# A four-layer graph network on one core: narrower one-hot groups, an integer addition moved to VectorE, and matrices placed inside a sum

## What is computed

```python
# 1: graph convolution: features = sum over edges of norm * (h @ W)[src]; then a small network
# 2: convolution with a matrix per edge
w = (relu(efeat @ W1 + b1) @ W2 + b2).reshape(E, 16, 16)
msg = einsum('ei,eio->eo', h[src], w)
agg = segment_sum(msg, dst) / max(deg, 1) + bias        # then relu and batch norm
# 3: sheaf layer: two Householder reflections per edge, messages to src and to dst
out = relu(x - sum_src(msg_s) - sum_dst(msg_d))
# 4: attention, 256 channels per edge
e1, e2 = (efeat @ W_msg + b_msg) * h[src], (efeat @ W_attn + b_attn) * h[src]
attn = softmax of e2 over the edges of one dst, per channel
ft = segment_sum(e1 * attn, dst).sum(axis=1)
```

## Time and profile before

| what | value |
|---|---|
| median of 3 runs | 9471.54 us (9471.53 to 9472.74) |
| the profiled execution: its time | 9465.25 us |
| the profiled execution: its span | 9463.5 us |
| mean granted clock of TensorE | 0.854 of 2.4 GHz |
| busy: TensorE, VectorE, GpSimd, ScalarE | 81%, 78%, 73%, 49% of the span |
| second convolution | about 1530 to 3270 us of the span |
| sheaf layer | about 3440 to 6025 us |
| attention | about 6135 to 9355 us |

### The profile page before, as it was taken

The page is one execution under the profiler, slowest core; times in us unless marked ns, Lnnn a source line. Parts: engine busy times, 40 slices in busy tenths (PEclk is TensorE's granted clock), DMA queues, the critical chain, the costliest instruction groups (busy, mean ns, idle before and its releaser), DMA issues. The chain is left out here.

```text
span 9463.5 us, 135509 instructions
## 1 busy us (share of the span) xinstructions
PE 7645.1 (81%) x35152; PEld 4283.9 (45%) x35152; DVE 7338.7 (78%) x11881; ACT 4606.7 (49%) x7496; POOL 6896.2 (73%) x6335
## 2 busy tenths in 40 slices
PE   3777774999999728888888888578888888888884
PEld 3666653555555415555555555333333333333331
DVE  6666653777777738888888888588888998988987
ACT  4666663667667416565655665323333333333333
POOL 6777776766666567777777777378777777777774
PEclk9888886777777659999999999789999999999997
DMA  4222211111111111111111111122222222222223
GB/s 147 55 52 53 55 46 36 42 41 40 42 41 40 34 17 32 31 27 31 31 27 31 31 31 21 18 62 72 77 72 71 72 71 75 75 71 72 71 74 99
DMA packets 498923, 493.19 MB, mean 52 GB/s; under 512 B 180303, under 2 KB 396134, under 8 KB 497959
## 3 DMA queue, kind: packets, MB, share of 16 engines
q1 hardware_dynamic: 298823, 371.60, 11.6%
q0 software_dynamic: 199904, 119.78, 9.1%
HBM read 240.96 MB, written 249.95 MB: 52 GB/s over the span
## 5 line engine op out<-in xcount | busy, mean ns | idle before, releaser
L2485 POOL DMA_INDIRECT attn_got<-tab,attn_line x1760 | 2152.3, 1223 | 648.7 <-issue 511.2
L1945 POOL DMA_INDIRECT sheaf_got<-tab,sheaf_idx x1612 | 1712.7, 1062 | 490.0 <-issue 472.5
L2538 PE MATMUL attn_q<-attn_X,ident 128*128 128x512 f32 x3520 | 1799.3, 658 | 1.8 <-DVE attn_X L2710 1.8
L2034 PE MATMUL sheaf_acc<-sheaf_hot_hi,sheaf_wide 128*128 128x392 bf16 x6696 | 1361.4, 346 | 272.1 <-DVE sheaf_hot_hi L2237 270.2
L1469 POOL DMA_INDIRECT nnconv_got<-tab,nnconv_idx x1116 | 1100.0, 986 | 456.0 <-issue 322.8
L1167 POOL DMA_INDIRECT gcn_got<-tab,gcn_idx x868 | 1018.9, 1174 | 301.4 <-issue 275.4
L2671 DVE TENSOR_TENSOR attn_T<-attn_w,attn_got 128x1024 f32<-128x1024 f32 x880 | 1035.0, 1218 | 246.4 <-PE attn_w L2529 206.6
L2538 PEld LDWEIGHTS attn_q<-attn_X,ident 128*128 128x128 f32 x3520 | 699.9, 210 | 1136.6 <-issue 1136.6
L2615 ACT COPY attn_S<-attn_q 128x512 f32<-128x512 f32 x440 | 255.9, 582 | 1624.4 <-PE attn_q L2545 1624.4
L2034 PEld LDWEIGHTS sheaf_acc<-sheaf_hot_hi,sheaf_wide 128*128 128x128 bf16 x6696 | 657.2, 106 | 809.2 <-issue 481.0
L2529 PE MATMUL attn_w<-src_hi 32*128 32x512 f32 x3520 | 586.5, 738 | 437.6 <-DVE attn_T L2671 436.7
(11 more groups left out here) (502 smaller groups left out, 13931.2 us busy)
## 6 DMA issues: line engine op xcount, KB each, us to landing
sums<-attn_S SPq DMA_DIRECT2D x110, 1024.0 KB, 4.2
tops<-attn_S SPq DMA_DIRECT2D x110, 512.0 KB, 2.9
attn_got<-tab,attn_line POOLq DMA_INDIRECT x1760, 2.6
sheaf_got<-tab,sheaf_idx POOLq DMA_INDIRECT x1612, 2.4
gcn_key<-src_key SPq DMA_DIRECT2D x62, 384.0 KB
gcn_blk<-src_blk SPq DMA_DIRECT2D x62, 384.0 KB
nnconv_got<-tab,nnconv_idx POOLq DMA_INDIRECT x1116, 2.4
nnconv_key<-src_key SPq DMA_DIRECT2D x62, 256.0 KB, 3.1
```

Of the source, the lines that this page charges most:

```text
L1945: e.indirect_dma_start(out=got[at.b][:, j, D:D + T2], out_offset=None, in_=tab[2], in_offset=indices(idx[at.b], j)).then_inc(s_got[half][a ...
L2034: mm = e.matmul(pacc[k][:, 0:HH], wide[at.b][half][:, part, col, :], hot[:, k * HH:(k + 1) * HH], start=False, stop=False, skip_group_chec ...
L2485: e.indirect_dma_start(out=got[at.b][:, 4 * q + n, :], out_offset=None, in_=tab[3], in_offset=indices(ids[:, q, n, :], D + 2)).then_inc(s_ ...
L2538: e.matmul(to, ident[:, :], X[:, q, :, n, :], start=n == 0, stop=False)
```

## The change

Three edits. In the second convolution the one-hot groups have GC = 3 columns instead of 4, so 6 columns come by one-hot and 20 are gathered, two more per block; all buffers, matmuls and copies of these groups are 384 instead of 512 wide, and each group picks 3 columns. The last part of the gathers is now columns 16 to 19. In the sheaf layer `ids_of` goes from GpSimd's program; VectorE adds the offset (NP times the mark) in `fixed`, behind each mark. In the attention TensorE issues the matrices of quad 0 two blocks ahead inside `quad_sum(at, 0)`, behind the third of the four positions. The diff, cut to its core:

```diff
@@ second convolution
         GN = 2
+        GC = 3
         BY_ACT = (NC, 4)
-        JN = J - GN * GW
+        JN = J - GN * GC
...
-            key = [sbl(f"key{b}", [P, GN, GW * P], F16) for b in range(2)]
-            blk = [sbl(f"blk{b}", [P, GN, GW * P], F16) for b in range(2)]
-            hot = [sbl(f"hot{q}", [P, NC, GW * P], F32R) for q in range(2)]
-            held = [sbl(f"held{q}", [P, GW * P]) for q in range(2)]
+            key = [sbl(f"key{b}", [P, GN, GC * P], F16) for b in range(2)]
+            blk = [sbl(f"blk{b}", [P, GN, GC * P], F16) for b in range(2)]
+            hot = [sbl(f"hot{q}", [P, NC, GC * P], F32R) for q in range(2)]
+            held = [sbl(f"held{q}", [P, GC * P]) for q in range(2)]
...
-                                mm = e.matmul(pacc[:, :],
+                                mm = e.matmul(pacc[:, 0:GC * P],
...
-                        for j in range(GW):
-                            at_col = q * GW * 2 * D + j * 2 * D
+                        for j in range(GC):
+                            at_col = q * GC * 2 * D + j * 2 * D
...
-                        e.copy(got[at.b][:, JN + g * GW:JN + (g + 1) * GW, :].rearrange("p j f -> p (j f)"),
-                               psel[:, q * GW * 2 * D:(q + 1) * GW * 2 * D]).then_inc(s_moved, 1)
+                        e.copy(got[at.b][:, JN + g * GC:JN + (g + 1) * GC, :].rearrange("p j f -> p (j f)"),
+                               psel[:, q * GC * 2 * D:(q + 1) * GC * 2 * D]).then_inc(s_moved, 1)
...
-                                               in1=pacc[:, :], op0=ALU.is_equal, op1=ALU.mult).then_inc(s_mask, 1)
+                                               in1=pacc[:, 0:GC * P], op0=ALU.is_equal, op1=ALU.mult).then_inc(s_mask, 1)
@@ sheaf layer, GpSimd
-                    def ids_of(at):
-                        turn_wait(e, s_ln[at.b], at.half(32 * NP2, 32 * NP2))
-                        for m in range(2):
-                            ids = line[at.b].bitcast(I32)[:, m, :, :, D + 2]
-                            e.tensor_tensor(ids, ids, void_src[:, bass.ds(at.of(2 * QB, m * QB), NP2), :],
-                                            ALU.add).then_inc(s_ids_part if m == 0 else s_ids, 1)
-
                     def step(at):
                         sources(at, 0)
-                        if 0 < at.k <= NBL:
-                            ids_of(at.plus(-1))
                         sources(at, 1)
@@ sheaf layer, VectorE
                         for m in range(2):
-                            e.tensor_copy(line[at.b][:, m, :, :, D + 1],
-                                          void[:, bass.ds(at.of(2 * QB, m * QB), NP2), :]).then_inc(s_mk, 1)
+                            quads_at = bass.ds(at.of(2 * QB, m * QB), NP2)
+                            ids = line[at.b].bitcast(I32)[:, m, :, :, D + 2]
+                            e.tensor_copy(line[at.b][:, m, :, :, D + 1], void[:, quads_at, :]).then_inc(s_mk, 1)
+                            e.scalar_tensor_tensor(out=ids, in0=void[:, quads_at, :], scalar=float(NP), in1=ids, op0=ALU.mult,
+                                                   op1=ALU.add).then_inc(s_ids_part if m == 0 else s_ids, 1)
@@ attention, TensorE
-                    def quad_sum(at, q):
+                    def quad_sum(at, q, between=None):
...
                         for n in range(4):
                             e.matmul(to, ident[:, :], X[:, q, :, n, :], start=n == 0, stop=False)
+                            if between and n == 2:
+                                between()
...
-                        quad_sum(at, 0)
-                        if at.k < NBQ - 2:
-                            matrices(at.plus(2), 0)
+                        quad_sum(at, 0, (lambda: matrices(at.plus(2), 0)) if at.k < NBQ - 2 else None)
```

## The result

The changed kernel takes 9229.65 us, the median of 3 runs (9218.75 to 9231.04), beside 9471.54 us before: a ratio of 0.9741, with a 95% interval of 0.9719 to 0.9763. That is 242 us faster. The forecast was 9246 us with a range of 9195 to 9350. The profiled execution has a span of 9227.9 us; it was 9463.5, so 235.6 us are to be found in the trace.

A forecast was written before the change was run, and what follows sets the result against it. Bounds: TensorE's chain in the convolution, GpSimd with VectorE just under it in the sheaf layer, VectorE's wait for matrices in the attention. Gains of 75 + 4 + 147 = 226 us from 9471.5 give 9246 us, range 9195 to 9350.

The forecast's parts named there:

- The block of 25.7 us: Second convolution: GpSimd's time per block after the change, twenty gathers at 1.275 us plus 0.2, making it the bound.
- 214 - 158: Second convolution: GpSimd's present waits, 214 us, less 158 us for two new gathers per block; a gain of 56 us.
- The lead: Second convolution: the last product starts 39 us after the last gather; this shrinks to some 15, 23 us more gain.
- reserve: Second convolution: ScalarE's 7.86 us of one-hot work lose up to 1.97, so TensorE's 1.54 us wait shrinks too; not counted.
- B: Rival: the convolution gains nothing, TensorE stays at its lower clock longer and remains the bound at 27.3 us; 9320, chance 0.14.
- D: Rival: slower, the clock never comes back in the convolution, 31.3 us per block against 27.3; 9568, chance 0.06.
- 24 x 0.34 = 8 us on the path: Sheaf layer: VectorE's added offsets cost 0.34 us in each of 24 blocks where it comes late out of the loop's turn.
- 0.53 us per block: Attention: VectorE's mean wait for TensorE's first matrices after the change, instead of 1.88 us.
- six take 5.0: Attention, slow block: six of eight TensorE records take 5.0 us before the moved matrices, which start at 8020.6.
- next limit: Attention: GpSimd's gathers, line fetches and what lies between, 3008 us or 27.34 per block, just below the forecast period of 27.6.
- Rival C: The attention gains little: TensorE is late with every later quad, or the clock falls there; up to 9392, chance 0.12.

The follow-up runs named there:

- version with the wait per quad: Changed kernel, but each attention product waits only for the product that read the same part of T two blocks before, not all four: 9211.84 us, ratio 0.9732.
- loaded version: The version with the wait per quad plus one idle GpSimd instruction (an iota) at the start of every attention block: 9237.98 us, ratio 0.9761.

## Why the prediction was right, and where its steps were off

The kernel is 242 us faster and the forecast had 226. Of the 16 us, 9 come from the three stages, 3 less than forecast in the convolution, 8 more in the sheaf layer and 4 more in the attention, 6 from the profiled execution of before, which lay under its median, and the rest from between the stages.

**Convolution, -75 against -72 (and -71 alone).** The reading was right: GpSimd held back, TensorE's chain the bound, and GpSimd the bound afterwards. Three details were not.

- The block of 25.7 us. "20 x 1.275 + 0.2" left out the 0.96 us between the copy of the indices and the first gather. Before, it ran inside GpSimd's waits for products and bias, and no row showed it. Instead of 56 us the end of the gathers moved by 41 (3227.6 to 3186.6). Both terms of "214 - 158" were off, in opposite directions. GpSimd's waits fell not by 214 us but from 220.7 to 60.2, which is all hand-over. And the new gathers cost not 158 us but 119: busy time rose from 1100.0 to 1184.2 and gaps from 322.8 to 358.0, as a gather takes 955 ns where it took 986. The difference, 160.5 - 119.4, is the 41 us.
- The lead. I had it shrink from 39 to 15 us; it shrank to 8 (3186.6 to 3194.4). So the two halves were 41 + 31 and not 56 + 19 to 23. That the sum comes so near is luck.
- Who waits. I named VectorE. It is ScalarE, whose bias copy is the first instruction that needs the last columns of a block, and TensorE behind it. ScalarE's 1.5 us less one-hot work (3.65 + 2.71 for 4.40 + 3.46) therefore did not shrink TensorE's idle time, my "reserve".

Rivals B and D did not come. The clock went from 0.75 to 0.73, and a selection and the matrices behind it still run at the lower level (1.49 and 2.08 us, where others of the same size take 0.85 and 1.13). But at 26.0 us per block TensorE still stands idle for 1.6 to 2.6 us. The Trainium skill ("TensorE: Matmul & The Clock Gate", Part 1) says that activity releases the throttle. The trace agrees: in the block above the slow sum takes 4.57 us, less than twice the 2.70 of the fast one, so the clock came back inside it, as it did before the change (5.90 against 3.53).

**Sheaf layer, -4 against -12 in the trace, and no difference alone.** VectorE's waits for gathers, 11.6 us, were the right thing to look for, and they are gone. From first to last message the three traces with the old layer (before, and the convolution and the attention alone) take 2521.6 to 2522.6 us, the eight with the new one 2504.8 to 2511.5. That is 10 to 18 us, so 11.6 was not the strict bound that it was taken for; what gives the rest was not followed up. The term that failed is "24 x 0.34 = 8 us on the path": the additions behind the loop's turn cost nothing that the stage shows. Whether the 12 us arrive in the whole time could not be shown; the interval of the kernel with this part alone, -12 to +5 us, holds both.

**Attention, -147 against -151 (-156 alone).** Right in kind. The wait that I left at 0.53 us per block is 0.15. The failed step is "six take 5.0" with a pass through the matrices of q = 3 at 2.09 us: from the end of TensorE's idle time to the start of the moved matrices I had 7.0 us, and there are 5.5 (7924.81 to 7930.34). They start 0.5 us after the product that frees them (7927.45 + 2.35), where I had 2.1. Even by my own figures six records with five slow ones are 5 x 0.85 + 0.46 = 4.7 us, not 5.0. What I missed on the other side is VectorE's own wait for X, 0.28 us per block, that the old wait had covered. 1.88 - 0.15 - 0.28 is 1.45 us per block, 158 us in 109 blocks; the trace has 151, because VectorE's busy time between first and last X rose by 8.5 us (2831.2 to 2839.7).

The "next limit", GpSimd at 27.34 us per block, was wrong in kind. After the change the same instructions take 26.05 us (2072.9 + 507.0 + 219.7 + 66.4 us over 110 blocks), and GpSimd waits 105 us for the lines. The version with the wait per quad has a block of 27.24 us, under the 27.34 itself. I had taken durations measured beside one course of VectorE for the engine's own. TensorE's idle time fell from 3.77 to 2.98 us, not to 2.4; nothing hung on it. Rival C did not come, but the place behind the second position shows that it stood close by: 54 us for one position.

## What to carry to other kernels

When an engine is made the bound, look for what it does inside the waits that go: the hand-over after a small copy is invisible there and is paid from then on. Where work is put inside a sequence, both sides count: too late, and its user waits; too early, and the engine waits for the buffer and everything behind it is late. And a sum of mean durations is a floor only for an engine whose instructions don't stretch beside others.

## What the runs showed of the hardware

**A small copy ahead of a gather costs 0.96 us, not 0.30.** Between two gathers lie 0.30 us; between GpSimd's copy of the indices (0.21 us) and the gather that reads them 0.95 and 0.96 us by the two lines shown, and 0.97 in the mean of 62 blocks. With the copy on ScalarE that gap is an ordinary one. Which part of it is the wait for the semaphore and which the change from a copy to a gather no run separates.

**Gathers stretch beside some VectorE instructions.** Most last 0.94 us. Some last 1.8 to 2.9, and one of these in the loaded version stands beside the instruction that combines two halves of `attn_T`. First GpSimd, then VectorE:

```profile
7913.50 0.94 POOL L2482 DMA_INDIRECT attn_got<-tab,attn_line  x1 [0.30 <-issue]
7914.75 2.80 POOL L2482 DMA_INDIRECT attn_got<-tab,attn_line  x1 [0.30 <-issue]
```

```profile
7913.32 1.21 DVE L2671 TENSOR_TENSOR attn_T<-attn_w,attn_got 128x1024 f32<-128x1024 f32 x1
7914.45 2.28 DVE L2686 SCALAR_TENSOR_TENSOR attn_two<-attn_T 128x2048 f32<-128x2048 f32 x1
```

The gather ends at 7917.55, 0.82 us after VectorE's instruction at 7916.73. The 0.94 us gather before it ran beside a product that reads one operand from `pw`, in TensorE's output memory. The pair stands for many. Between 6200 and 9090 us of this trace 105 gathers start while that combining instruction runs; they last 2.79 us in the mean, and each ends 0.81 to 0.82 us after it. 618 start while a product runs, and none lasts over 0.96 us. The Trainium skill ("SBUF — State Buffer", section "SBUF: two separate sides") says that VectorE with two inputs in SBUF and a GpSimd instruction that reads SBUF exclude each other for the whole instruction. The trace agrees with it, 2.80 for 0.94 us, if a gather counts as an instruction that reads SBUF, where its row numbers lie; no run separates that. It would explain why the mean gather of the attention moves between 1166 and 1223 ns from version to version, and why a load of 0.80 us on GpSimd is taken up in part. That the phase alone makes the difference was not tried by itself.

**TensorE's slower stretch after its idle time** moved without changing the sum. In the block of the changed kernel shown above the matrices of q = 3 take 1.25 us and the six records behind them 4.31; in one of the version with the wait per quad, after 2.98 us of idle time as well, they take 2.09 and 3.44:

```profile
7936.23 2.09 PE L2524 MATMUL attn_w<-src_hi 32*128 32x512 f32 x8 [2.98 <-DVE attn_T L2666]
7938.25 3.44 PE L2533 MATMUL attn_q<-attn_X,ident 128*128 128x512 f32 x6
```

That is 5.5 us both times, with parts of it at the lower of the two levels. It is not the version that moves it: another block of the changed kernel, at 7045.02, has 2.09 and 3.54.
